# A mixture-of-experts kernel: the second products of experts 6, 7 and half of 5 in three rounded products, and a new order around the last expert

## The chip, the cores and the metric

The kernel runs on one core of one Trainium2 chip. The metric is the device time of one execution in microseconds. Before the change it is 325.0 us (median of 3 runs, 324.57 to 325.73). Engines: PE is TensorE, DVE is VectorE, ACT is ScalarE, POOL is GpSimd, SP is SyncE, which only starts transfers here.

## The reference

```python
x = x + xattn(layernorm(x), ctx)      # 2 x 1024 rows of 256, 16 heads of 64, 64 context rows
                                      # logits and probabilities mixed over heads by Wth1, Wth2
x = x + ffn(layernorm(x))
# ffn: T = 2048 rows, E = 8 experts, C = T / E = 256 rows for each
scores = layer_norm(feat) @ centroids.T
for e in range(E):                    # balanced: the best C rows that no expert before took
    s = where(taken, -inf, scores[:, e]); idx = top_k(s, C); taken[idx] = True
h = layer_norm(routed)                # routed: expert e's rows, [E, C, 256]
h = gelu(einsum('ecd,edf->ecf', h, w1) + b1)   # 256 -> 1024
h = einsum('ecf,efd->ecd', h, w2) + b2         # 1024 -> 256
out = routed + h                      # back in the order of the rows
```

All inputs and outputs are float32.

## The kernel before

The attention fills the first 165 us or so; nothing in it changes. Its rows, normalised and not, lie in the DRAM tensor `rows_scratch`. From there on the eight experts are worked off in a software pipeline of slots k = 0 to 10 (`SLOTS`). In slot k three experts are under way:

- **Search for expert k.** Eight rounds find the score from which 256 rows are taken: DVE compares (`compare`), PE sums (`total`), DVE narrows (`narrow`). Then DVE and PE give every row its place (`select`, `ranks`). The last expert takes what is left and needs no search (`searches(k)` is false for k = 7); its `select` runs in round 3 of slot 7.
- **Rows of expert u = k - 1.** DVE makes the places into one-hot tensors (`slots`, `halves`, `one_hot`: `Hoh` and `Loh`), POOL multiplies one with the rows' numbers (`token_rows`: `Htk`), PE turns them into a list (`tokens`, 16 small products, and after ACT has copied it, `spread`), DVE reads the indices off (`indices`), POOL starts two gathers (`gather`: tile `G`), PE transposes the gathered rows (`rows`, two parts, in gaps 4 and 5), ACT scales them twice (`yF` as float32 and `yT` part 0 as float32r, a rounded form), POOL subtracts one from the other (`y_rest`: `yT` part 1). ACT and POOL make the same two parts of w1 (`w1_high`, `w1_rest`: `w1p`). The first products (`up`) are then, for each of 8 blocks f of 128 hidden columns and 2 of 128 input columns, three float32r products (`mm3`): high x high, high x rest, rest x high. Blocks 0 to 3 are done in gaps 8 and 9 of slot k.
- **Expert e = k - 2.** Blocks 4 to 7 of `up` (gaps 0 and 1), then the second products (`down`, gaps 2 to 7): for each half a of the 256 rows and each block f one float32 product of `hT` with `w2s`, 16 in all. ACT has made `hT` from PSUM with Gelu (`hidden`, one call for two blocks). `final` on DVE adds the rows in `G`, in round 5 for half 0 and in round 2 of the next slot for half 1; POOL scatters the result to the output (`scatter`, in slot e + 3).

Each engine runs its own list in the order written; semaphores are the only links. PE's order is written by hand: `expert_part(k, gap)` is called between the rounds with `UP_FIRST`, `UP_REST` and `DOWN`. Within a slot POOL's order is `token_rows`, a quarter of `w1_rest`, `gather`, three quarters of `w1_rest`, `y_rest`, `bias` (adds b2 to the rows in `G`), `scatter`. SP loads w1 of expert e + 1 when its buffer's rest has been made, and w2 of expert e when expert e - 2's second products are done, so w2 of expert 7 is asked for at the end of slot 7.

PE's clock was granted in full in every stretch of the expert stage. A float32 product stands in the profile as two instructions, a float32r product as one.

Of the kernel before, what the change touches and what calls it, by code (L numbers as in the profile page):

```python
# [11 lines left out]
P = 128  # L12
# [35 lines left out]
def build(nc, x, xT, ctxT, wqT, wk, wv, wo, wth1, wth2T, centT, gb, w1, b1, w2, b2, consts, iconsts, digits, out):  # L48
# [5 lines left out]
    with ExitStack() as top:  # L54
# [29 lines left out]
        xs = sb("xs", [P, T, C])  # L84
        xTs = sb("xTs", [P, CC, B * Q])
# [14 lines left out]
        sb("rest_of_factors", [P, 2 * B * CC * COLS + 2 * GROUPS * C - 2 * GB * ST * C - 5 * CC * CAP - 2 * FC * CAP])  # L100
# [87 lines left out]
        e_gT, e_yT, e_yl, e_h, e_hs = sem("rows_transposed"), sem("rowsT_copied"), sem("rowsT_rest"), sem("hidden_in_psum"), sem("hidden_made")  # L188
        e_o, e_rb, e_fin = sem("expert_out"), sem("residual_bias"), sem("rows_final")
# [38 lines left out]

        def par(t, u, lag):
            return (u - lag) % 2  # L230
# [4 lines left out]
        SLOTS = E + 3  # L235
        W1_PARTS = 4
# [141 lines left out]
        def _(pool):  # L378
# [139 lines left out]
            for k in range(SLOTS):  # L518
# [4 lines left out]
                if 0 <= e < E:  # L523
                    v = e % 2
                    token_rows(e)
                    if e > 0:
                        w1_rest(e, v, 0)
                    gather(e)
                    if e > 0:
                        for part in range(1, W1_PARTS):  # L530
                            w1_rest(e, v, part)
                    y_rest(e, v)
                    bias(e)
                if 0 <= k - 3 < E:
                    scatter(k - 3)
# [4 lines left out]
        def _(act):  # L540
# [128 lines left out]

            act.wait_ge(s_in["small"], 64)  # L670
# [3 lines left out]
            for k in range(SLOTS):  # L674
# [4 lines left out]
                if 0 <= u < E:  # L679
                    act.wait_ge(r_R, u + 1)  # L680
                    nc.scalar.activation(Rt[:], bank[3][0:LO, 0:LO], ACT.Copy).then_inc(r_Rt, 1)
# [7 lines left out]
                if 0 <= u < E:  # L689
                    rows(u, u % 2)  # L690
                    for g in range(first_part(u) // 2):
                        hidden(u, u % 2, g)

        @block.vector
        def _(dve):
# [326 lines left out]

            nc.vector.tensor_copy(M[:], S[:, 0, :].unsqueeze(1).to_broadcast([P, NT, T])).then_inc(r_m, 1)
            dve.wait_ge(r_init, 3)
            first_two()
            for k in range(SLOTS):
                u = k - 1
                if 0 <= u < E:
                    slots(u)
                    halves(u)  # L1030
                    one_hot(u, 1, Hoh, r_hoh)
                for r in range(ROUNDS):
# [7 lines left out]
                    if r == 0 and 0 <= u < E:  # L1040
                        one_hot(u, 0, Loh, r_loh)
                    if r == 1 and 0 <= u < E:
                        indices(u)
# [425 lines left out]
```

## Time and profile before

| | |
|---|---|
| median of 3 runs | 325.0 us |
| profiled execution | 324.3 us |
| its span | 322.5 us |
| PE busy | 289.0 us (90%) |
| DVE, ACT, POOL busy | 219.2, 145.3, 207.7 us |
| slots 2 to 6, each | 16.1 to 16.2 us |
| first `up` of expert 5, 6, 7 | 271.2, 286.3, 301.6 us |
| last second product ends | about 314.8 us |

The span runs from the first to the last record of the profiled execution; the device time holds 1.8 us more. Busy is the time that an engine works, as a share of the span.

### The profile page before, as it was taken

Reading aid. Unit: us, or ns where it says so; the run is one execution under the profiler, and the core shown is the slowest. Engines: PE = TensorE matmul, PEld = TensorE weight load, DVE = VectorE, ACT = ScalarE, POOL = GpSimd, SP = SyncE. Lnnn points to the kernel's source line nnn. Section 1 sums busy time; section 2 is a strip of 40 time slices with the busy share of each in tenths; the row PEclk is TensorE's granted clock in tenths of the full one; section 3 lists DMA queues with packets and bytes.
Section 4 is the critical chain, followed back from the end, with each engine's and each line's share of the span. In section 5 each row is a group of like instructions: output and inputs, shape, how many; then the busy total and the mean of one; then the engine's idle time right before and its main releaser. Section 6 shows DMA issues by size and latency. Waiting matters only on the chain.

```text
span 322.5 us, 6634 instructions
## 1 busy us (share of the span) xinstructions
PE 289.0 (90%) x2080; PEld 249.2 (77%) x2080; DVE 219.2 (68%) x742; ACT 145.3 (45%) x266; POOL 207.7 (64%) x287
## 2 busy tenths in 40 slices
PE   7999998999999999999811599999999999999990
PEld 4999887999989999999700267787878787878890
DVE  0679999788888887888538867878787878311000
ACT  1366564456545446655441244353535353532420
POOL 8200444468888888887855335758686868787831
PEclk9999999999999999999955599999999999999998
DMA  7993005930001000000112201645555655543010
GB/s 270 352 381 137 2 0 186 378 122 36 33 37 60 33 33 33 33 33 36 65 65 86 91 22 33 187 141 183 177 182 178 189 172 183 182 137 119 17 65 16
DMA packets 21768, 37.76 MB, mean 117 GB/s; under 512 B 2417, under 2 KB 14961, under 8 KB 21361
## 3 DMA queue, kind: packets, MB, share of 16 engines
q1 hardware_dynamic: 19184, 31.15, 28.0%
q0 software_dynamic: 2560, 6.31, 6.4%
q8 instruction: 13, 0.21, 0.3%
q14 instruction: 11, 0.08, 0.1%
HBM read 31.16 MB, written 6.29 MB: 116 GB/s over the span
## 4 chain that ended last, share of the span: by engine, by line
PE 72%; DVE 12%; issue 5%; POOL 5%; DMA 3%; ACT 2%; SPq 0%; POOLq 0%; DVEq 0%
PE pair L1058 63%; PE pair L1134 4%; DVE cmpb L919 3%; PE pair L1108 2%; DVE pair L952 2%; DMA wk_s<-wk_dram 2%; PE pair L1297 2%; POOL yT L499 1%; DMA G<-rows_scratch,idx 1%; POOL atleast L405 1%; PE pair L1146 1%; DVE sm L786 1%; DVE ok L939 1%; DVE wneg L707 1%; POOL sc L423 1%
## 5 line engine op out<-in xcount | busy, mean ns | idle before, releaser
L1058 PE MATMUL pair<-w2s,hT 128*128 128x256 f32 x256 | 63.2, 387 | 0.0
L1058 PE MATMUL pair<-yT,w1p 128*128 128x256 f32 x384 | 53.2, 288 | 1.6 <-POOL yT L499 1.6
L1058 PEld LDWEIGHTS pair<-yT,w1p 128*128 128x128 f32 x384 | 47.6, 188 | 4.3 <-issue 2.1
L1058 PE MATMUL pair<-Bm,pT 128*128 (+1 forms) x384 | 49.3, 283 | 0.2 <-ACT pT L580 0.2
L1058 PEld LDWEIGHTS pair<-w2s,hT 128*128 128x128 f32 x256 | 45.7, 191 | 4.6
L1058 PE MATMUL pair<-Am,xTp 128*128 (+1 forms) x192 | 48.9, 403 | 0.0
L1058 PEld LDWEIGHTS pair<-Bm,pT 128*128 128x128 f32 x384 | 46.1, 188 | 0.4 <-issue 0.4
L667 ACT ACTIVATE hT<-pair,b1s 128x256 f32<-128x256 f32 x64 | 26.9, 471 | 34.1 <-PE pair L1058 32.4
L493 POOL TENSOR_TENSOR w1p<-w1s,w1p 128x512 fp32r<-128x512 f32 x32 | 40.0, 1273 | 3.3 <-ACT w1p L646 3.1
L1058 PEld LDWEIGHTS pair<-Am,xTp 128*128 128x128 f32 x192 | 34.9, 188 | 7.4
L257 POOL TENSOR_TENSOR pr<-pr,rs 128x1024 f32<-128x1024 f32 (+1 forms) x16 | 31.2, 1950 | 14.0 <-DVE rs L793 12.7
L435 POOL TENSOR_TENSOR xTp<-xTs,xTp 128x256 fp32r<-128x256 f32 x16 | 11.9, 743 | 29.2 <-ACT xTp L547 29.1
L575 ACT ACTIVATE pr<-pr,r 128x1024 f32<-128x1024 f32 x16 | 18.4, 1150 | 25.2 <-DVE pr L835 25.2
L483 POOL DMA_INDIRECT G<-rows_scratch,idx x16 | 15.9, 992 | 16.6 <-DVE idx L1020 14.2
L657 ACT ACTIVATE yF<-pair,gbs 128x256 f32<-128x256 f32 x16 | 9.0, 564 | 35.8 <-PE pair L1297 35.8
L919 DVE TENSOR_SCALAR_CACHE_REDUCE cmpb<-pair 128x256 bf16<-128x256 f32 x48 | 23.5, 490 | 1.8
L1058 PEld LDWEIGHTS pair<-oh_b,cntb 128*128 128x128 bf16 x54 | 5.3, 98 | 24.0 <-DVE cmpb L919 22.8
L831 DVE TENSOR_REDUCE mx<-pair 128x16 f32<-128x1024 f32 x16 | 19.5, 1220 | 6.2 <-PE pair L1058 6.1
L514 POOL DMA_INDIRECT out_dram<-G,idx x16 | 15.8, 985 | 9.3 <-DVE G L959 5.9
L799 DVE TENSOR_TENSOR pT<-pair,pT 128x512 fp32r<-128x512 f32 x32 | 21.3, 669 | 0.4 <-ACT pT L580 0.4
L835 DVE TENSOR_TENSOR pr<-pair,mx 128x1024 f32<-128x1024 f32 x16 | 19.6, 1225 | 1.5
L1058 PE MATMUL pair<-oh_b,cntb 128*128 128x16 bf16 x54 | 9.9, 183 | 11.9 <-DVE cmpb L919 11.8
(146 smaller groups left out, 544.9 us busy)
## 6 DMA issues: line engine op xcount, KB each, us to landing
w1s<-w_dram SPq DMA_DIRECT2D x8, 1024.0 KB
w2s<-w_dram SPq DMA_DIRECT2D x8, 1024.0 KB, 7.8
rows_scratch<-row SPq DMA_DIRECT2D x16, 256.0 KB, 2.0
xs<-x_dram SPq DMA_DIRECT2D x1, 2048.0 KB, 17.1
xTs<-xT_dram SPq DMA_DIRECT2D x1, 2048.0 KB, 18.8
wk_s<-wk_dram SPq DMA_DIRECT2D x1, 1024.0 KB, 4.9
wv_s<-wv_dram SPq DMA_DIRECT2D x1, 1024.0 KB, 7.3
wqT_s<-wqT_dram SPq DMA_DIRECT2D x2, 512.0 KB, 8.6
```

The costliest lines, as they stand in the source:

```text
L257: return eng.tensor_tensor(p4, p4, rs[:, v, :].unsqueeze(1).unsqueeze(3).to_broadcast([P, end - first, H, K8]), ALU.mult)
L483: pool.indirect_dma_start(out=G[:, b, a, :], out_offset=None, in_=rows_dram, in_offset=bass.IndirectOffsetOnAxis(ap=idx[:, e, a:a + 1], ax ...
L493: nc.gpsimd.tensor_tensor(w1p[:, 1, v, c, half], w1s[:, v, c, half], w1p[:, 0, v, c, half].bitcast(f32), ALU.subtract).then_inc(e_w1l, 1)
L514: pool.indirect_dma_start(out=out, out_offset=bass.IndirectOffsetOnAxis(ap=idx[:, e, a:a + 1], axis=0), in_=G[:, b, a, C:], in_offset=None ...
L575: nc.scalar.activation(pr[:, v, :], pr[:, v, :], ACT.Exp, scale=r1[:, ds(t, 1)]).then_inc(s_exp, 1)
L667: nc.scalar.activation(hT[:, v, f, :], bank[1 + g % 2][:, h * CAP:(h + 1) * CAP], ACT.Gelu_apprx_tanh, bias=b1s[:, e * FC + f:e * FC + f + ...
L799: nc.vector.tensor_tensor(pT[:, 1, v, q], probs_bank(t, g)[:], pT[:, 0, v, q].bitcast(f32), ALU.subtract).then_inc(s_pTs, 1)
L831: nc.vector.tensor_reduce(mx[:, v, :], pair[v][:].rearrange("p (g i k) -> p i g k", i=H, k=K8), AX.XY, ALU.max).then_inc(s_mx, 1)
L835: nc.vector.tensor_tensor(pr[:, v, :].rearrange("p (g i k) -> p g i k", i=H, k=K8), pair[v][:].rearrange("p (g i k) -> p g i k", i=H, k=K8 ...
L919: nc.vector.tensor_scalar(cmpb[:], search_bank(k)[:, 0:T2 * P], thr.bitcast(f32), 0.0, ALU.is_ge, ALU.add, accum_out=cntb[:]).then_inc(r_c ...
L1058: return nc.tensor.matmul(out_, l, r, start=start, stop=stop)
L1134: last = nc.tensor.transpose(probs_bank(t, g)[:, j * P:(j + 1) * P], pr[:, v, q:q + P], ident)
```

## The change

Second products of blocks 4 to 7 of expert 5 and of all blocks of experts 6 and 7 (`parted`; `PARTED` = 5) are made by `mm3` from two float32r parts each of `hT` (tile `hp`) and of `w2s` (tile `w2p`): 40 float32 products become 120 float32r ones. The parts of w2 come in halves of 4 blocks: ACT rounds (`w2_high`, 128x1024), DVE subtracts (`w2_rest`, 128x1024). The parts of `hT` come for two blocks at a time, both from DVE: a copy that rounds and a subtraction (`hidden_split`, 128x512 each). `w2p` has two buffers and lies where the attention's inputs were, `hp` has one.

Around them the order changes. The list of expert 7 (`lists`, `one_hot`, `token_rows`, `tokens`, ACT's copy `lists_out`, `spread`, `indices`) moves from slot 8 into slot 7. POOL's `w1_rest` and `gather` of expert 7 move from the start of slot 8 to the end of slot 7, behind `y_rest` and `bias` of expert 6 and ahead of that slot's `scatter`: two quarters of the rest, the gathers, two quarters. PE takes `rows` of expert 7 one gap earlier (3 and 4).

```diff
+        w2p = sb("w2p", [P, 2, 2, FC, C], f32r)
+        hp = sb("hp", [P, 2, FC, CAP], f32r)
...
+        def parted(e, f):
+            return e > PARTED or e == PARTED and f >= FC // 2
+        def w2_parts(e, half):
+            return 1 if e == PARTED else 2 * (e - PARTED) + half
+        def hidden_parts(e, g):
+            return g - 1 if e == PARTED else FC // 2 * (e - PARTED) - 1 + g
         def par(t, u, lag):
             return (u - lag) % 2
...
         DRAIN = T
         SLOTS = E + 3
+        PARTED = E - 3
         W1_PARTS = 4
         def is_last(t):
...
                         w1_rest(0, 0, part)
                 if 0 <= e < E:
                     v = e % 2
-                    token_rows(e)
-                    if e > 0:
-                        w1_rest(e, v, 0)
-                    gather(e)
-                    if e > 0:
-                        for part in range(1, W1_PARTS):
-                            w1_rest(e, v, part)
+                    if e < E - 1:
+                        token_rows(e)
+                        if e > 0:
+                            w1_rest(e, v, 0)
+                        gather(e)
+                        if e > 0:
+                            for part in range(1, W1_PARTS):
+                                w1_rest(e, v, part)
                     y_rest(e, v)
+                    if e == E - 2:
+                        token_rows(E - 1)
                     bias(e)
+                    if e == E - 2:
+                        for part in range(W1_PARTS):
+                            if part == W1_PARTS // 2:
+                                gather(E - 1)
+                            w1_rest(E - 1, (E - 1) % 2, part)
                 if 0 <= k - 3 < E:
                     scatter(k - 3)
             for i in range(GB * ST):
...
                     nc.scalar.activation(hT[:, v, f, :], bank[1 + g % 2][:, h * CAP:(h + 1) * CAP], ACT.Gelu_apprx_tanh,
                                          bias=b1s[:, e * FC + f:e * FC + f + 1]).then_inc(e_hs, 1)
+            def w2_high(e, half):
+                act.wait_ge(e_w2[e % 2], 16 * (e // 2 + 1))
+                if e >= PARTED + 2:
+                    act.wait_ge(e_o, ST * (e - 1))
+                q = slice(half * FC // 2, (half + 1) * FC // 2)
+                nc.scalar.activation(w2p[:, (e - PARTED) % 2, 0, q], w2s[:, e % 2, q], ACT.Copy).then_inc(e_w2h, 1)
+            def lists_out(u):
+                act.wait_ge(r_R, u + 1)
+                nc.scalar.activation(Rt[:], bank[3][0:LO, 0:LO], ACT.Copy).then_inc(r_Rt, 1)
             act.wait_ge(s_in["small"], 64)
             act.wait_ge(s_sc, T)
             for v in range(2):
...
                 rest = range(first_part(e) // 2, FC // 2) if 0 <= e < E else ()
                 for g in rest[:1]:
                     hidden(e, e % 2, g)
-                if 0 <= u < E:
-                    act.wait_ge(r_R, u + 1)
-                    nc.scalar.activation(Rt[:], bank[3][0:LO, 0:LO], ACT.Copy).then_inc(r_Rt, 1)
+                if 0 <= u < E - 1:
+                    lists_out(u)
                 for g in rest[1:]:
                     hidden(e, e % 2, g)
                 if k < E:
...
                     nc.scalar.activation(mv2[:, 0, 0:1], wneg[:, 0:1], ACT.Gelu_apprx_tanh)
                 if 0 <= u < E:
                     rows(u, u % 2)
+                    if u > PARTED:
+                        w2_high(u, 0)
+                    if u >= PARTED:
+                        w2_high(u, 1)
                     for g in range(first_part(u) // 2):
                         hidden(u, u % 2, g)
+                        if u == E - 2 and g == 0:
+                            lists_out(E - 1)
         @block.vector
         def _(dve):
...
                     nc.vector.tensor_reduce(idx[:, k, :], Rx[:].rearrange("p (a b) -> p a b", a=ST), AX.X,
                                             ALU.add).then_inc(r_idx, 1)
+            def w2_rest(e, half):
+                dve.wait_ge(e_w2h, w2_parts(e, half))
+                q, b = slice(half * FC // 2, (half + 1) * FC // 2), (e - PARTED) % 2
+                nc.vector.tensor_tensor(w2p[:, b, 1, q], w2s[:, e % 2, q], w2p[:, b, 0, q].bitcast(f32),
+                                        ALU.subtract).then_inc(e_w2l, 1)
+            def hidden_split(e, g):
+                q = slice(2 * g, 2 * g + 2)
+                dve.wait_ge(e_hs, FC * e + 2 * g + 2)
+                if e > PARTED:
+                    dve.wait_ge(e_o, ST * e)
+                nc.vector.tensor_copy(hp[:, 0, q], hT[:, e % 2, q]).then_inc(e_hh, 1)
+                dve.wait_ge(e_hh, hidden_parts(e, g))
+                nc.vector.tensor_tensor(hp[:, 1, q], hT[:, e % 2, q], hp[:, 0, q].bitcast(f32), ALU.subtract).then_inc(e_hl, 1)
+            def lists(u):
+                slots(u)
+                halves(u)
+                one_hot(u, 1, Hoh, r_hoh)
             nc.vector.tensor_copy(M[:], S[:, 0, :].unsqueeze(1).to_broadcast([P, NT, T])).then_inc(r_m, 1)
             dve.wait_ge(r_init, 3)
             first_two()
             for k in range(SLOTS):
                 u = k - 1
-                if 0 <= u < E:
-                    slots(u)
-                    halves(u)
-                    one_hot(u, 1, Hoh, r_hoh)
+                if 0 <= u < E - 1:
+                    lists(u)
                 for r in range(ROUNDS):
                     counted = searches(k) and not (k == 0 and r < DIRECT)
                     if counted:
...
                             first_bits()
                         elif r > 0:
                             keep(k, r - 1)
-                    if r == 0 and 0 <= u < E:
+                    if r == 0 and 0 <= u < E - 1:
                         one_hot(u, 0, Loh, r_loh)
-                    if r == 1 and 0 <= u < E:
+                    if r == 0 and PARTED <= k - 2 < E:
+                        if k - 2 == PARTED:
+                            w2_rest(PARTED, 1)
+                        hidden_split(k - 2, 2)
+                    if r == 1 and 0 <= u < E - 1:
                         indices(u)
+                    if r == 1 and PARTED <= k - 2 < E:
+                        hidden_split(k - 2, 3)
                     if r == 2 and 0 <= k - 3 < E:
                         final(k - 3, 1)
                     if r == 3 and k == E - 1:
                         select(k)
+                        lists(k)
+                        one_hot(k, 0, Loh, r_loh)
                     if r == 5 and 0 <= k - 2 < E:
                         final(k - 2, 0)
                     if counted:
                         narrow(k, r)
                 if searches(k):
                     select(k)
+                if PARTED < u < E:
+                    w2_rest(u, 0)
+                    w2_rest(u, 1)
+                    hidden_split(u, 0)
+                    if u == E - 2:
+                        indices(E - 1)
+                    hidden_split(u, 1)
         @block.tensor
         def _(pe):
...
                 if f == 0 and e > 0:
                     pe.wait_ge(e_fin, ST * (e - 1) + a + 1)
                 if a == 0:
-                    pe.wait_ge(e_hs, FC * e + f + 1)
-                last = mm(bank[4 + a][:, 0:C], hT[:, v, f, a * P:(a + 1) * P], w2s[:, v, f, :], f == 0, f == FC - 1)
+                    if parted(e, f):
+                        pe.wait_ge(e_w2l, w2_parts(e, f // (FC // 2)))
+                        pe.wait_ge(e_hl, hidden_parts(e, f // 2))
+                    else:
+                        pe.wait_ge(e_hs, FC * e + f + 1)
+                if parted(e, f):
+                    last = mm3(bank[4 + a][:, 0:C], lambda i: hp[:, i, f, a * P:(a + 1) * P],
+                               lambda i: w2p[:, (e - PARTED) % 2, i, f, :], f == 0, f == FC - 1)
+                else:
+                    last = mm(bank[4 + a][:, 0:C], hT[:, v, f, a * P:(a + 1) * P], w2s[:, v, f, :], f == 0, f == FC - 1)
                 if f == FC - 1:
                     last.then_inc(e_o, 1)
...
             def list_of_tokens(k, gap, half):
                 u = k - 1
-                if gap == 1 and 0 <= u < E:
+                if gap == 1 and 0 <= u < E - 1:
                     if half == 0:
                         tokens(u)
                     else:
...
                     if searches(k) and not (k == 0 and r < DIRECT):
                         total(k, r)
                     if 0 <= u < E:
-                        if r in (4, 5):
-                            rows(u, r - 4)
+                        at = 3 if u == E - 1 else 4
+                        if r in (at, at + 1):
+                            rows(u, r - at)
                     if k == 1 and 2 <= r <= 6:
                         keep_busy()
                     if r == 3 and k == E - 1:
...
                 expert_part(k, 8)
                 if searches(k):
                     ranks(k)
+                if k == E - 1:
+                    tokens(k)
                 expert_part(k, 9)
+                if k == E - 1:
+                    spread(k)
                 if searches(k + 1):
                     spread_scores(k + 1)
```

## Rows read from the trace of the kernel before

**Rows 1.** The page's part 4, the whole span: the chain that ended last, by engine.

```profile
PE 72%; DVE 12%; issue 5%; POOL 5%; DMA 3%; ACT 2%; SPq 0%; POOLq 0%; DVEq 0%
```

**Rows 2.** Windows of slot 8 and slot 9: engine busy us (instructions), clock, DMA.

```profile
286.30:301.60 15.30, 14.58 (x102) 12.68 (x102) 1.37 (x5) 5.47 (x13) 12.37 (x13) 1.00 0.40 121
301.60:316.50 14.90, 12.99 (x80) 11.61 (x80) 1.01 (x3) 3.36 (x8) 7.92 (x9) 1.00 0.12 44
```

**Rows 3.** The chain of waits, slots 8 and 9: start, us, what.

```profile
294.05 3.46 DMA G<-rows_scratch,idx
...
301.62 0.74 POOL yT L499
```

**Rows 4.** Timeline of PE, 276 to 315 us: start, us, instructions, idle before.

```profile
276.62 0.56 PE L1058 MATMUL pair<-Htk,Loh 128*16 128x16 f32 x16
...
278.12 2.86 PE L1058 MATMUL pair<-w2s,hT 128*128 128x256 f32 x12
280.81 0.18 PE L1058 MATMUL pair<-GE,tri_b 128*128 128x32 bf16 x1
...
283.91 0.38 PE L1297 MATMUL pair<-cst,G 128*128 128x128 f32 x2
...
293.29 4.15 PE L1058 MATMUL pair<-w2s,hT 128*128 128x256 f32 x18
297.65 0.41 PE L1297 MATMUL pair<-cst,G 128*128 128x128 f32 x2 [0.21 <-DMA G<-rows_scratch,idx]
...
299.19 0.38 PE L1297 MATMUL pair<-cst,G 128*128 128x128 f32 x2
...
302.41 5.51 PE L1058 MATMUL pair<-yT,w1p 128*128 128x256 f32 x45 [0.23 <-POOL yT L499]
307.76 7.07 PE L1058 MATMUL pair<-w2s,hT 128*128 128x256 f32 x32
```

**Rows 5.** Timeline of DVE, slot 7.

```profile
274.94 0.41 DVE L1011 TENSOR_TENSOR Loh<-cst,pair 128x256 fp32r<-128x256 f32 x1
...
279.14 0.22 DVE L975 TENSOR_TENSOR_SCAN INC<-pair,GE 128x32 bf16<-128x32 f32 x1
```

**Rows 6.** Timeline of ACT, end of slot 7: last scaled rows, first Gelu of expert 6.

```profile
285.69 0.57 ACT L657 ACTIVATE yT<-pair,gbs 128x256 fp32r<-128x256 f32 x1
288.48 0.84 ACT L667 ACTIVATE hT<-pair,b1s 128x256 f32<-128x256 f32 x2 [2.22 <-PE pair L1058]
```

**Rows 7.** Timeline of POOL, slots 7 and 8.

```profile
275.57 0.64 POOL L474 TENSOR_TENSOR Htk<-Hoh,cst 128x256 fp32r<-128x256 f32 x1
...
278.88 1.01 POOL L483 DMA_INDIRECT G<-rows_scratch,idx  x1 [1.44 <-DVE idx L1020]
...
286.34 0.73 POOL L499 TENSOR_TENSOR yT<-yF,yT 128x256 fp32r<-128x256 f32 x1 [0.19 <-ACT yT L657]
287.03 1.42 POOL L507 TENSOR_TENSOR G<-G,b2s 128x256 f32<-128x256 f32 x2
...
296.35 3.71 POOL L493 TENSOR_TENSOR w1p<-w1s,w1p 128x512 fp32r<-128x512 f32 x3
```

**Rows 8.** Groups of instructions, whole span: busy, mean ns, idle before.

```profile
L799 DVE TENSOR_TENSOR pT<-pair,pT 128x512 fp32r<-128x512 f32 x32 | 21.3, 669 | 0.4 <-ACT pT L580 0.4
L835 DVE TENSOR_TENSOR pr<-pair,mx 128x1024 f32<-128x1024 f32 x16 | 19.6, 1225 | 1.5
...
L1023 DVE COPY M<-S 128x256 f32<-128x256 f32 x1 | 0.3, 317 | 0.0
...
L646 ACT ACTIVATE w1p<-w1s 128x2048 fp32r<-128x2048 f32 x8 | 15.2, 1905 | 2.3 <-DMA rows_scratch<-row 2.3
```

**Rows 9.** Group of POOL L257, then the one time that both engines run it.

```profile
L257 POOL TENSOR_TENSOR pr<-pr,rs 128x1024 f32<-128x1024 f32 x15 | 29.7, 1978 | 13.1 <-DVE rs L793 11.9 <-issue 1.1
...
152.14 0.69 DVE L257 TENSOR_TENSOR pr<-pr,rs 128x512 f32<-128x512 f32 x1
...
152.25 1.53 POOL L257 TENSOR_TENSOR pr<-pr,rs 128x512 f32<-128x512 f32 x1 [0.84 <-DVE rs L793]
```

More of the change, by code:

```diff
@@ L81, in build @@
         step_w = cst[:, C_W:C_W + ROUNDS * NT].rearrange("p (r j) -> p r j", r=ROUNDS)
-        xs = sb("xs", [P, T, C])
-        xTs = sb("xTs", [P, CC, B * Q])
+        with ExitStack() as inputs:
+            xs = sb("xs", [P, T, C], f32, inputs)
+            xTs = sb("xTs", [P, CC, B * Q], f32, inputs)
+        w2p = sb("w2p", [P, 2, 2, FC, C], f32r)
         wneg = sb("wneg", [P, HD // P])
@@ L99, in build @@
         hT = sb("hT", [P, 2, FC, CAP])
-        sb("rest_of_factors", [P, 2 * B * CC * COLS + 2 * GROUPS * C - 2 * GB * ST * C - 5 * CC * CAP - 2 * FC * CAP])
+        hp = sb("hp", [P, 2, FC, CAP], f32r)
+        sb("rest_of_factors", [P, 2 * B * CC * COLS + 2 * GROUPS * C - 2 * GB * ST * C - 5 * CC * CAP - 4 * FC * CAP])
         bst = sb("bst", [P, T, 6])
@@ L188, in build @@
         e_gT, e_yT, e_yl, e_h, e_hs = sem("rows_transposed"), sem("rowsT_copied"), sem("rowsT_rest"), sem("hidden_in_psum"), sem("hidden_made")
+        e_w2h, e_w2l, e_hh, e_hl = sem("w2_high"), sem("w2_rest"), sem("hidden_high"), sem("hidden_rest")
         e_o, e_rb, e_fin = sem("expert_out"), sem("residual_bias"), sem("rows_final")
```

## The prediction

> **What bounds the kernel now.** I read the chain that ended last first: 72% of it is PE [rows 1]. The windows of slots 8 and 9 show PE busy 14.58 of 15.30 us and 12.99 of 14.90 us at full clock (1.00, that is 2.4 GHz), POOL busy 12.37 and 7.92 us, and DVE idle (1.37 and 1.01 us) [rows 2]. So in slot 8 PE bounds and POOL is close behind. The chain shows where PE isn't alone: in slot 8 it runs through the gather for expert 7 (294.05, 3.46 us to landing), in slot 9 through POOL's subtraction at 301.62 [rows 3]. The timelines then give each engine's order.
>
> **Price of the products.** The last 16 float32 products of expert 7 are 32 records in 7.07 us: 0.442 us each. 45 float32r products of `up` run from 302.41 to 307.76, 5.35 us: 0.119 each, three of them 0.357 [rows 4]. The shapes are the same (128x128 by 128x256). A product of the new kind saves 0.085 us: 0.7 for 8 of expert 5, 1.4 each for experts 6 and 7, 3.4 us in all. That is the most that the products can give; the rest is what the parts and the new order cost.
>
> **Price of the parts.** ACT: 128x2048 takes 1.905, so 128x1024 some 1.05 [rows 8]. Last scaled rows of expert 6 end at 286.26, its first Gelu starts at 288.48 [rows 6]: 2.2 us idle, two halves of w2 (2.1) just fit. DVE: a subtraction is priced by its nearest rows, 0.669 for 128x512 and 1.225 for 128x1024, both with one input in PSUM [rows 8]. The rounding copy of 128x512: a copy of 128x256 took 0.317; a twice larger one at the pace of the subtractions (0.25 us more for 256 more) is 0.57 and never above their 0.67; at twice that pace it is 0.45. I take 0.45, being nearest to the copy's own row, and keep 0.45 and 0.67 as ends. So a `hidden_split` is 1.2 (1.15 to 1.4), an expert's eight blocks 4.8 us and its w2 2.45 us, 7.3 us on a DVE that is idle 13 us of the slot.
>
> **What they meet.** POOL has a row for this. 16 times it runs L257; 15 of them are 128x1024 at 1.978 us, so 128x512 should be near 1.1 (POOL's own 128x512 of w1: 3.71 / 3 = 1.24 [rows 7]). Once DVE runs the same line beside it, also from two SBUF inputs: DVE from 152.14 for 0.69, POOL from 152.25 for 1.53 [rows 9]. POOL took some 0.3 to 0.45 more; its work ends about 1.0 after DVE's end (152.83). I read it so: a POOL instruction that starts during such a DVE one works only when that is over, and ends at DVE's end plus its own time less 0.1; DVE, which was first, took its 0.69 as ever. What happens to DVE when POOL is first, no row shows. I take it that DVE goes on at its own speed; both other readings are rivals below. The Trainium skill (SBUF — State Buffer, Who interferes with whom) has the harder rule: a DVE instruction with two SBUF inputs and a POOL one that reads SBUF exclude each other for the whole instruction, whoever came first. Row and rule agree on POOL's side; by the rule the change would come out as the second rival does.
>
> **Slot 7.** `w2_rest` of expert 5 stands right behind `Loh`, so it runs from 275.3 to 276.5. POOL's `Htk` (start 275.57, 0.64) falls into it and ends near 277.0 instead of 276.2; PE reaches `tokens` at 276.62 and waits 0.45 [rows 4, 5, 7]. All of PE and the indices move by that: second products start at 278.57 (before 278.12), gathers at 279.35 (before 278.88). DVE then has split 2 (277.0 to 278.2), the indices (to 279.05), split 3, which waits for the last Gelu at 279.3 (to 280.5), then `final` and `select`, whose scan now ends at 281.4 (before 279.36). PE comes to `ranks` after 4 float32 and 2 new products, 278.57 + 1.77 + 0.71 = 281.05, and waits 0.35 [rows 4, 5]. Two new and one old product later, at 282.6, it waits for the first gather (279.35 + 3.46 = 282.8), does `rows`, three float32 products, and `rows` again at 284.35 (before 283.91 [rows 4]). From there ACT's four scalings and POOL's two subtractions lead to slot 8, and they are longer than the four products that PE has meanwhile. So expert 5's 0.7 us show nowhere, and slot 8 starts 0.45 late.
>
> **Slot 8.** `y_rest` of expert 6 ends at 287.5 (before 287.07). POOL has then `Htk` (0.6), two `bias` (1.42), two quarters of w1's rest (2.5) ahead of the gathers [rows 7]; alone it would be there at 292. DVE meanwhile: w2's halves 287.8 to 289.0 and 289.05 to 290.25, split 0 290.3 to 291.5, indices of expert 7 to 291.9, split 1 to 293.1 (Gelus are done before each). POOL: `Htk` to 288.15; `bias` held to 289.0, ends 289.6; held to 290.25, ends 290.85; w1's rest held to 291.5, ends 292.65; held to 293.1, ends 294.25. So the gathers are issued at 294.25, not earlier than before (294.05), and land at 297.7 and 299.05. PE finishes `up` at 293.74, does six new products (2.14), and stands from 295.9 to 297.8 for the first gather; three more products, second `rows` at 299.2 (before 299.19 [rows 4]). The new products' gain of that stretch is lost in the wait. Then 7 products in 2.5 us, to 302.0. POOL after the gathers (2.3 us, as from 294.05 to 296.35 [rows 3, 7]): 296.55, two quarters 2.5, the scatter of expert 4 2.3: 301.4; only then `y_rest` of expert 7, second part from 302.1 to 302.85. Before it ended at 302.36 [rows 3]. PE's full run of `up` starts at 302.9 instead of 302.41: 0.5 late.
>
> **Slot 9.** `up` ends at 308.25. DVE: w2's halves to 305.1 (ACT made them by 303.65), splits as Gelus come, split 2 to 309.1, split 3 (Gelu done 309.3) to 310.5. PE is at block 6 at 308.25 + 6 x 0.357 = 310.4 and waits 0.15; half 0 ends at 311.3, half 1 at 314.15, before 314.83. `final` of expert 6's second half now stands behind split 3 on DVE (310.9) and its scatter behind that; POOL is free and needs 1 us for it, before expert 7's first half at 312. The tail behind the last product (`final`, scatter, landing) is unchanged. The sum: + 0.5 at the start of `up` of expert 7, - 1.36 for its 16 products, + 0.15 for the wait: - 0.7 us. The profiled execution took 324.3 at a span of 322.5, 0.7 below the median; on the median of 325.0 I get **324.3 us**. This case's own range is 322.8 to 325.7.
>
> **Rival 1, nothing is held up.** The one row stands alone, and POOL's 1.53 may be its own time for that shape. Then slot 7 keeps its times (PE waits 0.3 at `ranks` and makes it good), the gathers for expert 7 go out at 291.6 (indices 291.3, POOL free 291.6), second `rows` at 296.5, POOL's scatter ends at 298.8 and `y_rest` at 300.2; `up` runs from 300.3 to 305.65, block 6 at 307.95 after split 3, end at 311.5: - 3.3, 321.7 us. For it: DVE and POOL both have the time [rows 2]. Against it: [rows 9].
>
> **Rival 2, slower: DVE and POOL exclude each other both ways.** Place: slots 7 and 8. DVE's copies and subtractions then also wait for POOL. Slot 7 ends 1.0 late (split 3 behind w1's rest, `select` behind it, gathers at 279.75). In slot 8, until the indices are there, POOL's 0.6 + 1.4 + 2.5 and DVE's 2.4 + 1.2 follow one another from 288.1: gathers at 295.5, split 1 to 296.5 (PE waits 1.5 for it), second `rows` at 300.4, POOL free at 303.2, `up` from 304.7, 2.3 late; slot 9 gives back 1.36 and loses 0.45 to late splits. + 1.4: 326.4 us. It decides once POOL's last `y_rest` ends more than 1.4 us later than before. For it: POOL is busy 12.37 of 15.3 us, so nearly every DVE instruction finds it at work [rows 2]. Against it: no row shows DVE waiting.
>
> **Rival 3.** The new products take as long as the old (weights of a second tile, more loads): then the case above ends 1.4 later, 325.7. The `up` products with the same pattern speak against it [rows 4]; 0.03.
>
> **Chances.** About 0.3% (1 us) is what a measurement tells from no change. The case of the sum 0.40, rival 1 0.27, rival 2 0.30, rival 3 0.03. Faster than 324.0: most of rival 1 (0.25), 0.16 of the sum's case, 0.01 of rival 2: 0.42. Within 324.0 to 326.0: 0.20 and 0.08: 0.28. Slower: 0.04, 0.21, and rival 3 with what is left: 0.30. Range for 8 in 10: 321.6 (rival 1) to 326.9 (rival 2 with the dearer copy).
>
> **What would show it.** Three new products in 0.36 us. `w2_rest` and the subtractions at 1.22 and 0.69 even beside POOL (my case), or up to 2.5 and 1.9 (rival 2); POOL's quarters of w1 over 1.3 us beside them, or 1.24 (rival 1). PE waiting for the gather at `rows` of expert 7 about 2 us, and 0.4 at `tokens` in slot 7. The gathers for expert 7 at 294.2, 291.6 or 295.5. I am wrong if POOL is late without DVE beside it, or if PE waits in slot 9 for more than the last split.

## The result, and the profile after

The change makes the kernel slower: 329.46 us median (329.0 to 329.57, 4 runs) beside 325.13 of the kernel before on the same chip, a ratio of 1.0125 (95% interval 1.0109 to 1.0141). I had forecast 324.3, with 326.9 as the upper end. Medians are of undisturbed executions: only the version all through PSUM (below) had others, two of its twelve, which took 370 and 477 us at a mean clock of 0.74 and 0.56.

I compare one stretch, from the first `up` product of expert 5 to the end of the last second product. Before it the two profiled executions differ in work that the change doesn't touch: PE's clock, which stands at 0.50 up to some 186 us in the kernel before as well (so it was not full in every stretch of the expert stage), was full some 2 us later, and the weights `wk_s` landed 5.9 us after issue, not 4.9, which makes the profiled execution after 1.44 us late at 272.65. The stretch itself took 43.62 us before and 47.49 after: +3.87. Behind it nothing changed.

Windows of the kernel before, cut at the first `up` of experts 5, 6 and 7: length, then busy us (instructions) of PE, PEld, DVE, ACT, POOL, then PE's granted clock, DMA share, GB/s.

```profile
271.21:286.28 15.07, 14.81 (x106) 12.80 (x106) 6.34 (x35) 7.27 (x14) 12.16 (x13) 1.00 0.53 181
286.28:301.60 15.32, 14.58 (x102) 12.70 (x102) 1.37 (x5) 5.47 (x13) 12.37 (x13) 1.00 0.39 121
301.60:314.83 13.23, 12.99 (x80) 11.61 (x80) 0.59 (x2) 3.36 (x8) 6.99 (x8) 1.00 0.14 50
```

The same windows of the kernel after:

```profile
272.65:289.00 16.35, 14.60 (x114) 12.95 (x114) 11.49 (x40) 7.94 (x16) 12.18 (x13) 1.00 0.49 168
289.00:308.35 19.35, 15.37 (x118) 14.27 (x119) 14.31 (x15) 9.02 (x17) 17.47 (x16) 0.91 0.31 96
308.35:320.14 11.79, 11.69 (x98) 11.31 (x96) 7.69 (x12) 3.44 (x9) 7.04 (x6) 1.00 0.16 58
```

Slot 7 is 1.3 us longer, slot 8 4.0, and slot 9 is 1.4 shorter. The sizes that stand out: in slot 8 POOL is busy 17.47 us with 16 instructions (12.37 with 13 before); DVE shows 14.31 us, where I had priced parts, splits and indices at 7.7 (two `final` and the first 0.85 us of expert 7's `w2_rest` are in the 14.31 too); and PE's clock is 0.91. [Rows 2] had full clock in both.

The page's chain by engine. Against [rows 1] DVE has gone from 12 to 17% and PE from 72 to 66%.

```profile
PE 66%; DVE 17%; issue 6%; POOL 4%; DMA 3%; ACT 2%; SPq 0%; ACTq 0%; POOLq 0%; DVEq 0%
```

Timeline of DVE after (start, us, instruction); the third line is two instructions in one:

```profile
276.71 3.26 DVE L1071 TENSOR_TENSOR w2p<-w2s,w2p 128x1024 fp32r<-128x1024 f32 x1
279.89 0.41 DVE L1080 CAST hp<-hT 128x512 fp32r<-128x512 f32 x1
...
289.94 3.17 DVE L1071 TENSOR_TENSOR w2p<-w2s,w2p 128x1024 fp32r<-128x1024 f32 x2 [4.28 <-ACT w2p L702]
...
294.02 1.67 DVE L1082 TENSOR_TENSOR hp<-hT,hp 128x512 fp32r<-128x512 f32 x1
...
299.31 3.52 DVE L1082 TENSOR_TENSOR hp<-hT,hp 128x512 fp32r<-128x512 f32 x1
```

Timeline of POOL after:

```profile
276.01 0.98 POOL L532 DMA_INDIRECT out_dram<-G,idx  x1 [0.31 <-issue]
277.01 0.64 POOL L492 TENSOR_TENSOR Htk<-Hoh,cst 128x256 fp32r<-128x256 f32 x1
277.59 1.29 POOL L511 TENSOR_TENSOR w1p<-w1s,w1p 128x512 fp32r<-128x512 f32 x1
...
290.32 3.39 POOL L525 TENSOR_TENSOR G<-G,b2s 128x256 f32<-128x256 f32 x2
293.67 3.17 POOL L511 TENSOR_TENSOR w1p<-w1s,w1p 128x512 fp32r<-128x512 f32 x2
...
298.29 1.47 POOL L501 DMA_INDIRECT G<-rows_scratch,idx  x1 [0.30 <-issue]
299.79 2.48 POOL L511 TENSOR_TENSOR w1p<-w1s,w1p 128x512 fp32r<-128x512 f32 x2
```

Read the two side by side. `w2_rest` of expert 5 (276.71, while POOL's scatter instruction of 276.01 was still running) shows 3.26 us for a length of 1.22. `Htk` and the quarter of w1 behind it run at their own pace (0.64; 1.29 against 1.24 in [rows 7]), and DVE ends at 279.97, 1.09 us after that quarter ended at 278.88: it did its work only then. The subtraction at 299.31 has 0.69 us of work, stands through two quarters of w1 that take their own 2.48, and ends at 302.83, 0.56 after them. In between the two take turns: `bias` 1.7 us each instead of 0.71, `w2_rest` 1.50 and 1.75, w1's quarters 1.47 and 1.74. So it goes both ways.

Timeline of PE after:

```profile
282.94 0.19 PE L1138 MATMUL pair<-GE,tri_b 128*128 128x32 bf16 x1 [0.70 <-DVE GE L1017]
...
285.07 0.41 PE L1377 MATMUL pair<-cst,G 128*128 128x128 f32 x2 [0.39 <-DMA G<-rows_scratch,idx]
...
298.00 2.03 PE L1138 MATMUL pair<-w2p,hp 128*128 128x256 f32 x12 [1.05 <-DVE hp L1082]
300.46 0.41 PE L1377 MATMUL pair<-cst,G 128*128 128x128 f32 x2 [0.43 <-DMA G<-rows_scratch,idx]
302.97 1.30 PE L1138 MATMUL pair<-w2p,hp 128*128 128x256 f32 x9 [2.11 <-DVE hp L1082]
304.11 0.45 PE L1377 MATMUL pair<-cst,G 128*128 128x128 f32 x2
304.25 4.26 PE L1138 MATMUL pair<-w2p,hp 128*128 128x256 f32 x21
308.35 5.81 PE L1138 MATMUL pair<-yT,w1p 128*128 128x256 f32 x48
314.00 6.14 PE L1138 MATMUL pair<-w2p,hp 128*128 128x256 f32 x48
```

PE stands twice for DVE's splits in slot 8, and then does 21 products in 4.1 us, 0.195 each, where 48 at the end take 0.128 each. The window of that stretch says why: the clock stood at 0.50, that is 1.2 GHz, behind the waits (before it fell, PE had been busy 4.3 of the 8 us from 296 to 304).

```profile
304.30:307.60 3.30, 3.30 (x18) 3.30 (x17) 0.17 (x2) 3.00 (x6) 2.41 (x4) 0.50 0.20 73
```

### The profile page after: what moved, and what is told of

It reads as the page before. It is cut to its first block, busy times and chain, and to the rows that moved or that the text cites. A ratio compares the mean times of both kernels' runs of the same rounds, so it can differ in the third digit from the quotient of the medians.

```text
span 327.8 us, 6773 instructions
## 1 busy us (share of the span) xinstructions
PE 289.3 (88%) x2119; PEld 250.9 (77%) x2120; DVE 244.4 (75%) x767; ACT 149.9 (46%) x271; POOL 212.8 (65%) x287
## 4 chain that ended last, share of the span: by engine, by line
PE 66%; DVE 17%; issue 6%; POOL 4%; DMA 3%; ACT 2%; SPq 0%; ACTq 0%; POOLq 0%; DVEq 0%
PE pair L1138 57%; PE pair L1214 4%; DVE cmpb L963 3%; PE pair L1188 2%; DVE hp L1082 2%; DVE w2p L1071 2%; DMA wk_s<-wk_dram 2%; DVE pair L996 2%; PE pair L1377 1%; DVE hp L1080 1%; POOL atleast L423 1%; DMA G<-rows_scratch,idx 1%; POOL out_dram L532 1%; PE pair L1226 1%; DVE sm L830 1%
## 5 line engine op out<-in xcount | busy, mean ns | idle before, releaser
L1138 PE MATMUL pair<-w2s,hT 128*128 128x256 f32 x176 | 45.0, 390 | 0.0
L1138 PEld LDWEIGHTS pair<-w2s,hT 128*128 128x128 f32 x176 | 30.9, 191 | 2.8
L532 POOL DMA_INDIRECT out_dram<-G,idx x16 | 16.8, 1052 | 7.8 <-DVE G L1003 4.7
L1138 PE MATMUL pair<-w2p,hp 128*128 128x256 f32 x120 | 18.0, 303 | 3.4 <-DVE hp L1082 3.2
```

The costliest lines, as they stand in the source:

```text
L532: pool.indirect_dma_start(out=out, out_offset=bass.IndirectOffsetOnAxis(ap=idx[:, e, a:a + 1], axis=0), in_=G[:, b, a, C:], in_offset=None ...
L1138: return nc.tensor.matmul(out_, l, r, start=start, stop=stop)
```

## The experiments

The theory: DVE's new instructions, above all those that read two SBUF inputs, and POOL's shut each other out, in both directions, and that alone turns the change into a loss. Rivals: the new order, the part of expert 5, or the copies and parts as such (more work on DVE and ACT, more loads on PE).

**The same work without the second SBUF input.** The second input of every new DVE instruction is a constant in PSUM (the copy, which had one input, becomes a multiplication by it); the rests are therefore not computed, and the output is not the reference's.

```diff
-  tensor_tensor(w2p[:, b, 1, q], w2s[:, e % 2, q], w2p[:, b, 0, q].bitcast(f32), ALU.subtract)
+  tensor_tensor(w2p[:, b, 1, q], w2s[:, e % 2, q], psum_one([P, FC // 2, C]), ALU.subtract)
-  tensor_copy(hp[:, 0, q], hT[:, e % 2, q])
+  tensor_tensor(hp[:, 0, q], hT[:, e % 2, q], psum_one([P, 2, CAP]), ALU.mult)
-  tensor_tensor(hp[:, 1, q], hT[:, e % 2, q], hp[:, 0, q].bitcast(f32), ALU.subtract)
+  tensor_tensor(hp[:, 1, q], hT[:, e % 2, q], psum_one([P, 2, CAP]), ALU.subtract)
```

> The changed kernel, but the second operand of DVE's new instructions is a constant in PSUM: w2_rest and both steps of hidden_split read one SBUF tensor each and keep their element counts (the copy becomes a multiplication by one, some 0.67 us instead of 0.43). The rests are not computed, so the output is not the reference's. From the first product of expert 5 to the end of the last one is 43.6 us before and 47.5 after. Theory H (DVE's two-input instructions and copies and POOL's instructions hold each other up): w2_rest 1.22 us each instead of 1.5 to 3.3, POOL's bias and w1 rests back at 0.73 and 1.27, the stretch is 40.5 to 41.5 us and the time 322 to 323.5 us. Rival O (the new order or the mere amount of new DVE work costs it): the stretch stays within 1 us of 47.5, time 328.5 to 329.5 us.

Measured: 322.46 us beside 325.25, ratio 0.9922 (0.9897 to 0.9946). From its DVE, POOL and PE timelines and its windows, cut as above:

```profile
275.94 1.22 DVE L1075 TENSOR_TENSOR w2p<-w2s,pair 128x1024 fp32r<-128x1024 f32 x1
```

```profile
288.22 1.43 POOL L525 TENSOR_TENSOR G<-G,b2s 128x256 f32<-128x256 f32 x2
```

```profile
297.91 2.63 PE L1144 MATMUL pair<-w2p,hp 128*128 128x256 f32 x21
300.48 6.11 PE L1144 MATMUL pair<-yT,w1p 128*128 128x256 f32 x48
```

```profile
271.70:286.90 15.20, 14.50 (x114) 12.96 (x114) 10.28 (x41) 7.94 (x16) 12.17 (x13) 1.00 0.54 182
286.90:300.48 13.58, 13.13 (x117) 12.44 (x118) 8.77 (x14) 7.55 (x16) 12.56 (x14) 1.00 0.44 137
300.48:313.10 12.62, 11.99 (x97) 11.41 (x96) 8.45 (x12) 4.89 (x10) 6.75 (x8) 1.00 0.15 54
```

The same order, and each instruction has its own length: 1.22 and 0.71 us. POOL is back at 12.56 us in slot 8, the slot at 13.58, the clock at 1.00. Of the subtractions only the second SBUF input is gone, and the copy has become a longer instruction (0.69 instead of 0.43) that is not held either. So the hold between DVE and POOL, that of the copies included, is the whole loss: (1.0125 - 0.9922) x 325 = 6.6 us. The run also shows what became of the +3.87. PE's busy time over the three windows is 42.38 before, 41.66 after, 39.62 here, its idle time 1.24, 5.83 and 1.78. After against before: +4.6 of waits, -2.8 of products and order (42.38 to 39.62), and +2.0 (39.62 to 41.66) that the same instructions took longer. Of these 2.0 us, 1.5 are the 21 products at the low clock: 4.10 us to the next line there, 2.57 here. The rest I can't assign.

**Only the new order** (`PARTED = E`: no product in parts; expert 7's `indices` are called where the change has them).

```diff
-        PARTED = E - 3
+        PARTED = E
```

> The changed kernel with PARTED = E: all second products in float32, no parts made; what is left is the new order of expert 7's list, gathers, w1 rest and rows. Theory H: the order by itself gains, since GpSimd doesn't wait for expert 7's indices any more: the stretch from expert 5's first product to the last one's end is 42.3 to 43.0 us (before 43.6), time 324.0 to 324.6 us if the start is as before. Rival O: GpSimd's scatter of expert 4 now stands ahead of y_rest, the stretch is 45 us or more, time over 326.5 us. Rival S (the 1.4 us that the changed kernel is late already at slot 7 belong to its code or layout, not to chance): first product of expert 5 at 272.6 us here too.

Measured: 323.9 beside 325.25, ratio 0.9957 (0.9941 to 0.9973); stretch 42.30. The gathers for expert 7 went out at 291.94, 20.55 us after the first `up` of expert 5, where the kernel before has 294.05 [rows 3] and 22.84, and `up` of expert 7 needs no wait. The order is worth 1.3 us by itself and isn't the culprit.

**Only the parts** (the old order of expert 7's list, gather, w1 rest and `rows`).

```diff
-                    if e < E - 1:
-                        token_rows(e)
...
+                    token_rows(e)
```

> The changed kernel's parts and products with the order of before (list, gathers, w1 rest, rows of expert 7 where they were). Theory H: the holding stays, and expert 7's indices now stand behind expert 6's third split on DVE; stretch 46 to 49 us, time 328 to 331 us. Rival O: the loss was in the order, stretch 43.6 or less, time 325 us or less.

Measured: 328.69 beside 325.25, ratio 1.0109 (1.0074 to 1.0144), stretch 46.7. The held `w2_rest` is there too (276.04, 3.26 us). Slot 8's wait has another place, PE's `tokens`, and the low clock follows it: 27 products in 4.66 us to the next line, 0.17 each.

```profile
296.36 0.58 PE L1124 MATMUL pair<-Htk,Loh 128*16 128x16 f32 x16 [2.34 <-POOL Htk L492]
...
297.97 4.82 PE L1124 MATMUL pair<-w2p,hp 128*128 128x256 f32 x27
302.63 0.38 PE L1363 MATMUL pair<-cst,G 128*128 128x128 f32 x2
```

**Only expert 7 in parts**, with the new order; slot 9 has a POOL that no one waits for.

```diff
-            return e > PARTED or e == PARTED and f >= FC // 2
+            return e > PARTED
-        PARTED = E - 3
+        PARTED = E - 2
```

> New order, but only expert 7's 16 products are made in three. DVE's new instructions then fall only at the end of slot 8 and in slot 9. Theory H: gathers for expert 7 at about 291.5 to 292.5, as without holding; w2_rest meets bias only; stretch 41.2 to 42.2 us (order 1.0, products 1.2 less), time 323 to 323.7 us. Rival O: over 46 us, as in the changed kernel, time over 327 us.

Measured: 323.09 beside 325.25, ratio 0.9934 (0.9912 to 0.9956), stretch 41.3. The hold is there all the same, and costs nothing: DVE's two `w2_rest` show 3.28 us together (2.35 without the hold) and POOL's two `bias` 2.41 (1.43), while PE runs through. Timelines of DVE and PE:

```profile
301.66 3.28 DVE L1071 TENSOR_TENSOR w2p<-w2s,w2p 128x1024 fp32r<-128x1024 f32 x2 [3.13 <-ACT w2p L702]
```

```profile
301.39 5.96 PE L1138 MATMUL pair<-yT,w1p 128*128 128x256 f32 x48
307.18 6.14 PE L1138 MATMUL pair<-w2p,hp 128*128 128x256 f32 x48
```

**The change without expert 5's part** (`parted` returns `e > PARTED`, with `PARTED` left at 5; the calls for expert 5 go).

> The changed kernel without expert 5's part (its 16 products in float32, no parts made in slot 7). Prices that part. Slot 7 grew by 1.26 us in the changed kernel. Theory H: w2_rest of expert 5 is held 2.0 us and takes the splits, indices and gathers of slot 7 with it; without it slot 7 is as before (15.1 us from first product to first product) and the stretch 46.2 us, time 327.5 to 328.5 us. If slot 8's loss came from slot 7's lateness, the stretch would be below 45.

Measured: 327.82 beside 324.78, ratio 1.0097 (1.0079 to 1.0115), stretch 46.2. Slot 7 is 15.11 us long, as before. Slot 8 is that of the change, wait for wait: PE 1.05 and 2.08 us for DVE, DVE's last split 3.52 us, then 21 products in 4.1 us. Timeline of PE:

```profile
295.39 2.03 PE L1136 MATMUL pair<-w2p,hp 128*128 128x256 f32 x12 [1.05 <-DVE hp L1082]
...
300.37 1.30 PE L1136 MATMUL pair<-w2p,hp 128*128 128x256 f32 x9 [2.08 <-DVE hp L1082]
```

So the two slots add up; expert 5 is the smaller part (1.3 us of the stretch), expert 6 the larger.

**Experts 6 and 7 with Gelu's result in PSUM**, from where DVE copies and subtracts; `w2_rest` still has two SBUF inputs. ("As above" in the forecast means the version all through PSUM, which stands next.)

```diff
-                nc.scalar.activation(hT[:, v, f, :], bank[1 + g % 2][...], ACT.Gelu_apprx_tanh, ...
+                to = bank[6 + g % 2][:, h * CAP:(h + 1) * CAP] if e > PARTED else hT[:, v, f, :]
+                nc.scalar.activation(to, bank[1 + g % 2][...], ACT.Gelu_apprx_tanh, ...
```

> As above, but only the hidden values go through PSUM; w2's rests are still subtracted from two SBUF inputs, four of them, and the scatter of expert 4 stands where the changed kernel has it. Theory H: two w2 rests (1.1 us of hold each) before the gathers for expert 7 make POOL about 2 us late there, the copies and subtractions nothing; stretch 42.6 us (changed kernel 47.5, without any holding about 41.3), time 324.4 us. If the copies and subtractions of hidden values held nothing up, it would be 45 or more.

Measured: 324.95 beside 324.78, ratio 1.001 (0.9991 to 1.0029), stretch 43.8, forecast 42.6. Against the run without expert 5's part (46.2) that is 2.4 us less. The splits ran unheld (0.68 and 0.69), the clock stayed at 1.00; what is left is `w2_rest` against `bias`, which delays the gathers (22.5 us after the first `up` of expert 5, 20.45 with expert 7 alone in parts), and in slot 9 the splits. Timelines of POOL and PE:

```profile
288.77 3.38 POOL L525 TENSOR_TENSOR G<-G,b2s 128x256 f32<-128x256 f32 x2
```

```profile
298.19 0.41 PE L1381 MATMUL pair<-cst,G 128*128 128x128 f32 x2 [1.27 <-DMA G<-rows_scratch,idx]
```

**All through PSUM:** ACT also copies w2 to PSUM ahead of `w2_rest`, and expert 4's first scatter moves behind `y_rest` of expert 7.

```diff
-  nc.vector.tensor_tensor(w2p[:, b, 1, q], w2s[:, e % 2, q], w2p[:, b, 0, q].bitcast(f32),
+  nc.scalar.activation(pair[3][:].rearrange(...), w2s[:, e % 2, q], ACT.Copy)
+  nc.vector.tensor_tensor(w2p[:, b, 1, q], pair[3][:].rearrange(...), w2p[:, b, 0, q].bitcast(f32),
```

> New order, all 32 products of experts 6 and 7 in three (expert 5's in float32), and no DVE instruction with two SBUF inputs and no copy from SBUF to SBUF: ACT's Gelu writes to PSUM banks 6 and 7, which the searches no longer use, and DVE rounds and subtracts from there; ACT also copies w2's halves there, DVE subtracts ACT's rounded part. The scatter of expert 4 moves behind y_rest of expert 7. Theory H: POOL's instructions keep 0.73 and 1.27 us, gathers for expert 7 as in the kernel with expert 7 alone (20.4 us after the first product of expert 5), the stretch from that product to the end of the last is 40.3 us (41.3 there; before 43.6), time 322.1 us. Rival: without holding it is ACT's added calls that bind, Gelu of expert 6 or its scaled rows come late; stretch 42 us or more, time 323.5 or more.

Measured: 323.8 beside 324.78, ratio 0.9977 (0.9959 to 0.9995), stretch 42.7 and not 40.3. Nothing is held any more: DVE 1.22 and 0.69, POOL 1.43 for two `bias`; but a new wait came up in slot 9. So the rival of this forecast had the size (42 us or more) but not the cause: ACT's last Gelu waited for none of the engines, as far as the profile shows ("remote"). Timelines of ACT and PE:

```profile
308.32 0.81 ACT L701 ACTIVATE pair<-pair,b1s 128x256 f32<-128x256 f32 x2 [2.33 <-remote]
```

```profile
310.73 3.77 PE L1159 MATMUL pair<-w2p,hp 128*128 128x256 f32 x30 [2.07 <-DVE hp L1105]
```

**The same with a shorter list for ACT.** A load of instructions (0.01 MB) fell into that wait; I tried whether the length of ACT's list sets its place.

```diff
-                q = slice(half * FC // 2, (half + 1) * FC // 2)
-                nc.scalar.activation(w2p[:, (e - PARTED) % 2, 0, q], w2s[:, e % 2, q], ACT.Copy).then_inc(e_w2h, 1)
+                nc.scalar.activation(w2p[:, (e - PARTED) % 2, 0], w2s[:, e % 2], ACT.Copy).then_inc(e_w2h, 1)
```

> The kernel whose new DVE work goes through PSUM, with a shorter program for ACT only: one call of 128x2048 for a whole w2 instead of two of 128x1024, and a dozen waits less that others cover. In its longer form the stretch was 42.7 us instead of the forecast 40.3; ACT's last Gelu waited 2.3 us where the trace has an instruction load of 10 KB (307 to 308 us), and PE waited 2.07 us for it. Theory L (ACT waited for its code): with a shorter program the load falls elsewhere, the last Gelu starts 1.4 us after the one before, stretch 40.7 to 41.1 us, time 322.2 to 322.7 us. Rival W (the wait was one for DVE's parts or for a bank): same wait again, stretch 42.5, time 324 us.

Measured: 324.2 beside 325.2, ratio 0.9975 (0.9953 to 0.9997). The wait stood at the same Gelu, 2.25 us: this idea fell.

**All through PSUM, with the scatter back in its place** ahead of `y_rest` of expert 7.

```diff
-                if 0 <= k - 3 < E and k != E - 1:
-                    if k == E:
-                        scatter(k - 4)
+                if 0 <= k - 3 < E:
```

> The all-PSUM kernel with one thing undone: expert 4's first half is scattered ahead of y_rest of expert 7 again, where the change has it. In the all-PSUM kernel and in its shorter-ACT form the last Gelu of expert 7 came 2.3 us late (at 308.3 and 308.0, released by something outside the core's engines), while POOL issued five scatters in a row from 302.5 to 308.6 and a load of instructions of 0.01 MB fell into 307 to 308. POOL stood idle for 2.2 us ahead of y_rest there, so the scatter (1.0 us and 0.3 of issue) should cost the path at most 0.3 us. Theory S (the row of scatters delays that load): four scatters, the wait goes; stretch 42.7 - 2.1 + 0.3 = 40.9 us, 322.2 us in all. Theory N (the load comes at that point of ACT's program whatever POOL does): the last Gelu still waits about 2.3 us and PE 2.0 behind it; stretch 42.7 to 43.0, 324.0 us.

Measured: 322.71 beside 325.07, ratio 0.992 (0.9906 to 0.9933), stretch 41.2. ACT's last Gelu waits for PE alone, 0.83 us and not 2.33, and PE 0.57 us, not 2.07; the 1.5 us are the difference of the two stretches:

```profile
307.37 0.81 ACT L699 ACTIVATE pair<-pair,b1s 128x256 f32<-128x256 f32 x2 [0.83 <-PE pair L1157]
```

Three scatters stand in a row there (303.06 to 306.58), not five, and four in a row held up no Gelu in the kernel before (303.89 to 308.71). So the place of that one scatter made the wait, as the forecast had it; that it is the length of the row is likely, not shown. How it does it stays open too: the small load of instructions is here as well, after 308, when that Gelu is done, so it isn't shown that the load was what the scatters delayed. With the same products in parts and nothing held, the stretch is 41.2 us, where the run without expert 5's part had 46.2. About 2.4 us of the difference were the splits' hold and about 2.6 that of `w2_rest`.

**When does DVE get its turn?** Two runs of the change put fills on DVE ahead of expert 5's `w2_rest`, one of 0.27 us and two of 0.66 together, so that it would meet another instruction of POOL.

```diff
+                            nc.vector.memset(ok1[:], 0.0).then_inc(r_init, 1)
```

> The changed kernel with one fill of 256 elements (0.3 us) ahead of DVE's w2_rest of expert 5, which was held for 2 us: it started 0.3 us before the end of a scatter instruction of POOL and ended 1.1 us after the two instructions that followed it on POOL, which ran at their own pace. Theory A (a DVE instruction that starts beside POOL's DMA instruction is passed over until POOL pauses): started 0.3 us later, inside POOL's Htk, it takes its turn after that one, some 1.7 us long, and POOL's w1 rest is held instead (2.3 us instead of 1.29). Theory B (POOL's back-to-back run always goes first): it ends as before, 1.1 us after POOL's w1 rest, some 2.9 us long.

> The changed kernel with two fills (0.5 us) ahead of DVE's w2_rest of expert 5. With one fill it started in the same 10 ns as POOL's Htk and was still held to 1.1 us after POOL's w1 rest. Now it starts in the middle of Htk. Theory A (it takes its turn at the end of the POOL instruction it found running): 1.4 to 1.6 us long, POOL's w1 rest 2.3 us. Theory B (a back-to-back run of POOL goes first): 2.6 us long, w1 rest 1.29.

Measured: 328.87 and 328.62 us (one run each). First run, DVE and POOL:

```profile
276.32 2.97 DVE L1071 TENSOR_TENSOR w2p<-w2s,w2p 128x1024 fp32r<-128x1024 f32 x1
```

```profile
276.33 0.64 POOL L492 TENSOR_TENSOR Htk<-Hoh,cst 128x256 fp32r<-128x256 f32 x1
276.91 1.29 POOL L511 TENSOR_TENSOR w1p<-w1s,w1p 128x512 fp32r<-128x512 f32 x1
```

In the second run `w2_rest` began at 276.41 inside `Htk` (276.03 to 276.66) and ended at 278.99, 1.09 after the quarter of w1 (277.90). Wherever it began, it came after both of POOL's instructions. A rule "DVE has its turn after the one instruction that it met" is false here; "a run of POOL instructions without a gap goes first" holds in slot 7, but in slot 8 DVE (289.94, inside `Htk` again) had its turn before `bias`. What decides is open. The fills also moved the instructions of slot 8, and there the one that stood through POOL's two quarters of w1 was a copy: 3.12 and 3.11 us instead of 0.42.

**The best version again.** Expert 7 alone in parts, with the new order.

> New order, expert 7 alone in three products, as run before (323.1 us, ratio 0.9934), once more beside the kernel above, so that the two are compared on the same chip. Theory L: 0.4 to 0.8 us slower than the kernel above; rival W: 0.9 faster than it.

Measured: 322.49 us beside 325.2, ratio 0.9918 (0.9901 to 0.9935), stretch 41.3. It is 0.8% faster than the kernel before and 1.7 us faster than the version with a shorter list for ACT (324.2), beside which it was run, so that the forecast's rival W holds. The version through PSUM (0.992) gains no more from 16 more products in parts.

## Why the prediction was wrong

The step that failed stands in "What they meet": "I take it that DVE goes on at its own speed". I had one row, with DVE first [rows 9], and took the harmless reading for the case that it didn't show. The run with the PSUM operand settles it: with DVE's second input out of SBUF the same change is 0.9922 of before, with it 1.0125. The Trainium skill (SBUF — State Buffer, Who interferes with whom), which I had set beside the sum and not into it, is borne out in both directions (DVE 1.22 to 3.26, POOL 0.71 to 1.72). The Trainium skill's sentence there, "Issue order, not op shape, decides who blocks", is not enough: `w2_rest` began 0.3 us before `Htk` (with only the scatter instruction running on POOL) and yet came after it and the next one.

Point by point:

- **Price of the products**: too high. The last 16 take 6.14 us (7.07 in [rows 4]), 0.058 less each and not 0.085: 2.3 us for 40, not 3.4. By PE's busy time, 41.74 with the order alone against 39.62 with the PSUM operand, it is 2.1. I had taken old products end to end and new ones start to start.
- **Price of the parts**: right. ACT 1.06 (1.05); copy 0.43 (0.45); subtraction 0.69; `w2_rest` unheld 1.22.
- **Slot 7**: forecast 0.45 late, measured 1.3. `tokens` didn't wait, since POOL went first; DVE's chain did: `w2_rest` to 279.97, the indices, gathers at 281.60, `select` late, and so waits of 0.70 at `ranks`, 0.39 at `rows` and 0.59 at `y_rest` (0.28 before; 0.59 also with the PSUM operand, so this one isn't the hold's). The form is rival 2's ("ends 1.0 late").
- **Slot 8**: forecast 0.05 later than slot 7's delay, measured 3.6 (4.0 by the windows, but before, the first three `up` of expert 7 stood apart by a wait of 0.47 that falls into slot 9). I had one wait of 1.9 us at the gather; it was 0.43, and the waits were for DVE's splits, 1.05 and 2.11.
- **Slot 9**: forecast -1.2, measured -1.0 by the same count. POOL has nothing there that PE needs, as I had it.
- **Rival 1** (321.7) is ruled out by the rows, but its time is near to what the work costs without the hold: 322.46. **Rival 3**: the products are faster.
- **Rival 2** had the mechanism, both slots and the sign, and its point of decision was passed (`y_rest` of expert 7 ends 3.6 us later in the stretch, over 1.4). It was too small by some 2.5 us in the stretch. It let the two engines alternate, instruction by instruction; a single DVE instruction was passed over for 2.0 and 2.8 us. And it had no term for PE's clock, which fell behind the waits: 1.5 us. No case of the prediction had one.

My chance of 0.30 for it was too low: the stated rule of the Trainium skill against a row that didn't contradict it should have outweighed "no row shows DVE waiting", and the kernel before shows the two meeting only once.

## What to carry to other kernels

Before new work goes to an idle vector engine, count its SBUF inputs and lay it against the other engine's list: with two of them it costs its own length and POOL's, on both. One input in SBUF isn't safe either: the copies were held too (0.95 to 3.12 us instead of 0.42). Put one input in PSUM (same 1.22 and 0.69 us here, but ACT's copy of each half of w2 to PSUM took 1.03 more, and a copy out of PSUM 0.68), or put the work where nobody waits for either engine, as in the last slot. And price a wait of PE with what the clock takes behind it: 21 products in 4.1 us instead of 2.57.

## What the runs showed of the hardware

- The clock's fall doesn't follow from one wait's length: PE stood 2.07 us at 310.73 in the run with all through PSUM and the clock stayed at 1.00; it fell behind 2.34 us with the old order, and behind 1.05, 0.43 and 2.11 close together in the change.
- DVE's copy, with one SBUF input, is drawn in too: 0.95 and 1.23 us instead of 0.42 beside POOL's work, 3.12 in the run with one fill (0.68 from PSUM, never held). And POOL's issue of a gather took 1.47 us instead of 0.96 beside one.
- A copy to float32r of 128x512 takes 0.42 us out of SBUF and 0.68 out of PSUM; the subtraction 0.69 from either.
- With five scatters issued back to back ACT's last Gelu came after a wait of 2.33 us, with three after one of 0.83 (for PE). Four in a row in the kernel before held up no Gelu.
